# A decoder of twelve sublayers on one core: scan outputs summed by TensorE, l3's attention lagged, l2's down products in one block, statistics where x is completed, latent folds by transposes

## The reference

```python
def _layernorm(x, axis=-1, eps=1e-05):
    m = jnp.mean(x, axis=axis, keepdims=True)
    v = jnp.var(x, axis=axis, keepdims=True)
    return (x - m) / jnp.sqrt(v + eps)

# L1_attn: a selective scan over 256 positions, 96 channels, 16 states
def step(x, inp):
    dA_t, dBu_t, C_t = inp
    x = dA_t * x + dBu_t
    y = jnp.einsum('bdn,bn->bd', x, C_t)
    return (x, y)
# ... the result is y + u * Dp

# L2_xattn, L3_xattn: 16 heads of latent attention. The weights alone give, head by head,
# a matrix Am (Wq, w_kc_q, W_qr, W_kr) for the queries and Bm (w_kc_kv, Wo) for the outputs.
```

## Time and profile before

| | |
|---|---|
| device time, median of 3 runs | 3240.33 us (3240.13 to 3252.0) |
| the profiled execution | 3245.44 us, its span 3243.6 us |
| TensorE / VectorE / ScalarE / GpSimd busy | 78% / 55% / 30% / 25% |
| mean granted TensorE clock | 0.829 of full |
| layer norms start at (us) | 7, 129, 274, 493, 731, 1158, 1296, 2116, 2444, 2565, 2713, 3039 |
| l1 attention; its scan | 493 to 731; 578.6 to 722.4 |
| folds of l2's and l3's latent attention | 2126.5 to 2170.2; 2723.9 to 2767.5 |
| l2 feed-forward's down products | 2534.7 to 2564.8 |
| l3 attention, from first scores to last addition | 2601.5 to 2713.2 |

### The profile page before, as it was taken

How to read it: one execution, slowest core, us unless ns; L and a number is a source line. 1 busy time by engine, 2 the same in 40 slices (tenths; PEclk the granted TensorE clock), 3 DMA queues, 4 the chain that set the end, 5 groups by cost and what they waited for, 6 DMA issues and landing times. The chain is left out here.

```text
span 3243.6 us, 37597 instructions
## 1 busy us (share of the span) xinstructions
PE 2533.6 (78%) x14342; PEld 1696.4 (52%) x14342; DVE 1770.8 (55%) x3533; ACT 985.2 (30%) x2219; POOL 814.6 (25%) x586
## 2 busy tenths in 40 slices
PE   7784443668999979569778697779998666999899
PEld 4563321224345556448666475765558545555555
DVE  5347586994455533674847657425556544355411
ACT  3131011541045521233342343405552011355311
POOL 1210001220058832100100000007880000488322
PEclk8886555669999989687978788779999856999899
DMA  1000000003000010210000001030001003000311
GB/s 32 20 16 20 0 1 13 0 0 98 1 1 1 1 53 1 107 24 1 14 14 13 14 1 26 1 91 1 1 1 39 19 1 91 1 1 1 96 44 37
DMA packets 96554, 72.86 MB, mean 22 GB/s; under 512 B 51232, under 2 KB 89936, under 8 KB 95801
## 3 DMA queue, kind: packets, MB, share of 16 engines
q1 hardware_dynamic: 95353, 69.01, 7.6%
q0 software_dynamic: 1024, 1.45, 0.2%
HBM read 65.17 MB, written 5.28 MB: 22 GB/s over the span
## 5 line engine op out<-in xcount | busy, mean ns | idle before, releaser
L1964 POOL TENSOR_SCALAR work<-work,small 128x512 f32<-128x512 f32 x384 | 594.0, 1565 | 809.1 <-DVE small L1900 809.1
L1942 ACT ACTIVATE work<-psum,small 128x512 f32<-128x512 f32 x384 | 260.5, 683 | 251.9 <-DVE small L1895 251.9
L1895 DVE TENSOR_REDUCE small<-psum 128x2 f32<-128x1024 f32 x192 | 234.9, 1225 | 179.0 <-PE psum L1845 178.9
L1845 PE MATMUL psum<-keysT,arena_a 64*128 64x512 f32 x768 | 218.2, 647 | 9.1 <-ACT work L1942 6.2
L1855 PEld LDWEIGHTS psum<-consts,work 128*128 128x128 f32 x1536 | 164.9, 141 | 114.3 <-issue 102.5
L1867 PE MATMUL psum<-work,keys 128*64 128x256 f32 x1536 | 187.0, 384 | 36.1 <-issue 34.2
L1855 PE MATMUL psum<-consts,work 128*128 128x128 f32 x1536 | 211.1, 280 | 4.4 <-DVE work L1906 2.6
L1867 PEld LDWEIGHTS psum<-work,keys 128*64 128x64 f32 x1536 | 120.0, 136 | 136.0 <-issue 110.0
L2753 PE MATMUL psum<-xnT,arena_a 128*128 128x256 f32 x512 | 154.7, 463 | 29.3 <-DVE arena_b L3133 29.3
L1489 PE MATMUL psum<-arena_b,arena_a 96*96 96x512 f32 x128 | 93.3, 898 | 71.9 <-DVE arena_b L1518 37.5
L2753 PEld LDWEIGHTS psum<-xnT,arena_a 128*128 128x128 f32 x512 | 117.0, 236 | 55.9 <-DVE arena_b L3133 31.5
(11 more groups left out here) (582 smaller groups left out, 5122.7 us busy)
## 6 DMA issues: line engine op xcount, KB each, us to landing
arena_a<-in_L_xattn_Wo SPq DMA_DIRECT2D x3, 2048.0 KB, 13.4
arena_a<-in_L_xattn_Wq SPq DMA_DIRECT2D x3, 2048.0 KB, 18.2
arena_a<-in_L_xattn_w_kc_q SPq DMA_DIRECT2D x3, 1536.0 KB, 12.8
arena_a<-in_L_attn_w_qkv SPq DMA_DIRECT2D x1, 4096.0 KB
arena_a<-in_L_xattn_W_qr SPq DMA_DIRECT2D x3, 768.0 KB
arena_b<-in_L_ffn_w_fc SPq DMA_DIRECT2D x1, 2048.0 KB
arena_b<-in_L_ffn_w_proj SPq DMA_DIRECT2D x1, 2048.0 KB
arena_a<-in_L_attn_w_gate SPq DMA_DIRECT2D x1, 2048.0 KB
```

The source lines that it names most:

```text
L1845: mm = nc.tensor.matmul(ps[:, u % 2 * 2 + j, :], qT[r:r + DC, p, t * P:(t + 1) * P], k.keysT[r:r + DC, b * SK:(b + 1) * SK], start=True, s ...
L1895: nc.vector.tensor_reduce(top[:, 2 * u:2 * u + 2], ps[:, u % 2 * 2:u % 2 * 2 + 2, :], AX.X, ALU.max, negate=True).then_inc(*maxed.up())
L1942: nc.scalar.activation(probs[u % NPB][:, j, :], ps[:, u % 2 * 2 + j, :], ACT.Exp, bias=top[:, i:i + 1], accum_out=total[:, i:i + 1]).then_ ...
L1964: nc.gpsimd.tensor_scalar(probs[u % NPB][:, j, :], probs[u % NPB][:, j, :], total[:, i:i + 1], None, ALU.mult).then_inc(*scaled.up())
```

## The change

1. `statistics` takes the statistics of a tile right behind the addition that completes it, in the block of the sublayer before; `layernorm` starts with the aggregation (the first stage keeps its own).
2. In l1's scan TensorE sums the sixteen products and u * D into two PSUM banks by an identity matrix; GpSimd's block is gone. B and C columns are spread one by one over three pairs of banks.
3. In the folds without rope Dm and Am are made transposed, with 64-column weights and 128 or 256 columns streamed, and turned by 8 and 16 transposes. w_qc loads in the layer norm, w_kc_kv and Wo last, and Bm is made last.
4. l2's down products move into the block of the steps; additions take two tiles at once.
5. l3's loop is lagged by one more item for transposes and sums, with three buffers for the probabilities. ScalarE takes the copy of the transposed probabilities and the squares; VectorE weighs the sums as it takes them from PSUM. Root, scaling and output projection follow in the same block by pairs of tiles. The lambda steps come first in the projection block.

```diff
+def statistics(k, dve, tiles, done):
+    dve.wait_ge(*done)
+    for t in tiles:
+        k.nc.vector.bn_stats(k.ln_stats[:, t, :], k.x[:, t, :]).then_inc(*k.sig("ln_stats").up())
 def layernorm(k, interleave=False, fetch=None, first=False):
-            for t in range(NT):
-                last = nc.vector.bn_stats(st[:, t, :], x[:, t, :])
-            k.link(dve, last, "dve")
+            if first:
+                for t in range(NT):
+                    nc.vector.bn_stats(st[:, t, :], x[:, t, :]).then_inc(*k.sig("ln_stats").up())
+            dve.wait_ge(k.sig("ln_stats").sem, k.sig("ln_stats").total)
...
 # l1_attn, scan, TensorE
+            def spread(r):
+                s, g = divmod(r, 2)
+                if r >= 3:
+                    pe.wait_ge(*(read if (r - 3) % 2 else taken).at((r - 3) // 2 + 1))
+                w = w_x[:, R + g * NS + s:R + g * NS + s + 1].broadcast_to([C, C])
+                for n in range(2):
+                    mm = nc.tensor.matmul(ps[0:C, r % 3 * 2 + n, :], w, u[:, n * 512:(n + 1) * 512], start=True, stop=True)
+                mm.then_inc(*bred.up())
+            def collect(s):
+                if s >= 0:
+                    pe.wait_ge(*read.at(s + 1))
+                for n in range(2):
+                    mm = nc.tensor.matmul(ps[0:C, y_banks[n], :], k.c["ident"][0:C, 0:C], hC[s % 2][:, n * 512:(n + 1) * 512],
+                                          start=s < 0, stop=s == NS - 1)
+                mm.then_inc(*added.up())
+            for r in range(2):
+                spread(r)
+            collect(-1)
             for s in range(NS):
...
+                for r in (2 * s + 2, 2 * s + 3):
+                    if r < 2 * NS:
+                        spread(r)
+                collect(s)
-        @block.gpsimd
-        def _(pool):
-            for s in range(NS):
-                pool.wait_ge(*read.at(s + 1))
-                nc.gpsimd.tensor_tensor(y, y, hC[s % 2], ALU.add).then_inc(*added.up())
-                pool.wait_ge(*added.at(s + 1))
+            dve.wait_ge(*added.at(NS + 1))
+            nc.vector.tensor_copy(y.rearrange("p (a b) -> p a b", a=2), ps[0:C, 6:8, :])
...
 # latent_attention, folds without rope, TensorE
+                for hp in range(HP):
                     for c in range(2):
-                        mm = nc.tensor.matmul(ps[:, h // 8, h % 8 * DC:(h % 8 + 1) * DC], w_qc[:, h, c, :],
-                                              Cm[:, c_at(h), c, :], start=c == 0, stop=c == 1)
+                        for j in range(2):
+                            h = 2 * hp + j
+                            mm = nc.tensor.matmul(ps[j * DC:(j + 1) * DC, 4 + hp // 4, hp % 4 * K:(hp % 4 + 1) * K],
+                                                  Cm[:, c_at(h), c, :], w_qc[:, h, c, :], start=c == 0, stop=c == 1)
+                pe.wait_ge(*taken.at(2))
+                for hp in range(HP):
+                    mm = nc.tensor.transpose(ps[:, 6 + hp // 4, hp % 4 * P:(hp % 4 + 1) * P], DmT[:, hp, :], k.c["ident"])
                 pe.wait_ge(*taken.at(3))
-                        mm = nc.tensor.matmul(ps[:, 2 + col // 512, col % 512:col % 512 + DC],
-                                              wq[:, h, c * P:(c + 1) * P], Dm[:, h, :], start=True, stop=True)
+                    mm = nc.tensor.matmul(ps[r:r + DC, hp // 2, hp % 2 * D:(hp % 2 + 1) * D], Dm[:, h, :], wq[:, h, :],
+                                          start=True, stop=True)
+                pe.wait_ge(*taken.at(4))
...
+                outputs(0)
...
 # l2_ffn, TensorE, after the steps and in their block
+            pe.wait_ge(*used.at(len(steps) - 1))
+            for t in range(NT):
+                pe.wait_ge(*ready.at(t // 2 * 2 + 2))
+                for j in range(G * R):
+                    mm = nc.tensor.matmul(ps[:, t // 2, t % 2 * D:(t % 2 + 1) * D], hs[:, j // R, j % R, t * P:(t + 1) * P],
+                                          wd[:, j // R, j % R, :], start=j == 0, stop=j == G * R - 1)
...
 # l3_attn, the loop: TensorE, ScalarE, VectorE
-            for m in range(M + 2):
+            for s in range(M + 3):
+                if s < M:
+                    scores(s)
+                if 2 <= s <= M + 1:
+                    turn(s - 2)
+                if s >= 3:
+                    over_keys(s - 3)
+            for b in range(B + 1):
+                if b < B:
+                    turn_out(b)
+                if b >= 1:
+                    project(b - 1)
...
+            for s in range(M + 4):
+                if s < M:
+                    exps(s)
+                if 2 <= s <= M + 1:
+                    keep(s - 2)
+                if s >= 4:
+                    square(s - 4)
+            nc.scalar.activation(ss, ss, ACT.Sqrt, bias=k.c["eps5"], scale=1.0 / HW).then_inc(*rooted.up())
+            for b in range(B):
+                keep_out(b)
...
+            for s in range(M + 3):
+                if s < M:
+                    row_max(s)
+                if 1 <= s <= M:
+                    mix(s - 1)
+                if s >= 3:
+                    weigh(s - 3)
```

267 lines of the change are left out of this document (145 added, 122 removed).

## The result

The changed kernel takes 3124.3 us (median of 4 runs, 3117.0 to 3126.2) against 3244.2 us before on the same chip: a ratio of 0.9624, 95% interval 0.9597 to 0.9650. The prediction was 3120 us. The profiled execution took 3123.0 us, its span is 3121.2 us and the mean granted clock 0.855 (before 0.829).

The account below looks back on a forecast made before the run. No single bound was taken: each changed stretch was priced by the wait that ends last. Savings of 9.7 + 17.3 + 31.4 + 18.8 + 43.2 = 120.4 us off 3245.4, less 5.1 to the median, gave 3120 us (3095 to 3145).

Parts of the forecast that it names:

- l2's down products: l2's feed-forward: down products run under VectorE's last two steps and end at 2545.3 instead of 2564.3, saving 18.8 us.
- l3's attention: l3's attention: the lag cuts an item from 5.74 to 3.15 us; with the lambda steps moved, 43.2 us saved.
- Layer norms: Eleven layer norms start with the aggregation: 8 save 2.16 us and 3 save 2.75, 25.5 us in all.
- the last pairs: Statistics behind the last additions before each layer norm lie on the path, costing 8.8 us in all.
- I expose a third: Inner statistics steps in l0 and l2 attention and three latent stages: a third counted as unhidden, 4 us.
- Scan: l1's scan: without GpSimd's addition a step falls from 8.55 to 7.4 us; 17.3 us saved in sum.
- rival (1): l1's scan: TensorE at half clock becomes the bound, a step takes 10.3 us, kernel 3188 us; chance 0.07.
- Rival (4): l1's scan: L200 is long for another reason than GpSimd's addition; 18 us more, kernel 3138 us; chance 0.02.
- Folds: Latent-attention folds in l2 and l3: each falls from 43.7 to 28 us, 31.4 us saved for both.
- rival (2): Latent-attention folds: only they stay at half clock, 36.3 us instead of 28, kernel 3136 us; chance 0.10.
- Rival (3): l3's loop: squares between exponentials cost ScalarE two table switches an item; 22 us more, kernel 3142 us; chance 0.05.
- Rival (5): Latent loops: delayed by statistics, they keep a longer rhythm; at 0.68 us a unit the kernel takes 3250; chance 0.02.

Follow-up runs that it names:

- stats_ln: The changed kernel with all statistics steps put back at the start of the layer norms: 3121.0 us, ratio 0.9624.
- beside: The changed kernel with an unread GpSimd addition of 96x1024 put beside each of the first fifteen scan steps: 3127.5 us, ratio 0.9647.
- l0_late: The changed kernel with the statistics of a pair in l0's attention moved behind the next gating in VectorE's queue: 3104.6 us, ratio 0.9580.
- l3_fill: l0_late with two needless products of 128 rows and 256 columns per item in l3's attention loop, ahead of the sums: 3098.7 us, ratio 0.9564.
- warm_all: l0_late with four needless 512-column products on TensorE at the start of every layer norm but the first: 3115.1 us, ratio 0.9604.

## Why the prediction was right, and where it wasn't

The total (3120 against 3124.3) is right, in part by luck. Of its terms four are right or nearly so. Stepping from before over stats_ln to the changed kernel, by the profiles: scan, folds with the queries, down products and l3's attention gave 115.6 us (110.7 forecast), everything else 10.9 (none forecast, 9.9 of them in the delta rule), the statistics -4.1 (9.7 forecast): 122.4, where 120.4 was forecast. Errors of 14 us one way and 16 the other met in the middle.

- **Layer norms.** 25.5 us forecast, 24.9 measured; the table load is late next, as stated, and takes 1.28 us.
- **What the statistics cost elsewhere: mis-sized in one block, missed in two, open in sum.** I counted 8.8 for the last pairs and 7 for the inner steps. Against stats_ln 28 us came back by the medians and 25 by the ratios, not 15.8, so the net of 9.7 came out as 0 to -3; by the three other kernels with the same steps it is 9 to 11. Where I costed a step by its own duration I was right: l0's feed-forward lost 2.7 (3.2). The step that failed is "I expose a third": in l0's attention three steps of 0.8 us stand ahead of the gating, and TensorE, arriving later, gets the half clock more often. They mostly cost 6 to 8 us between the first addition and the last, where a third would be 0.8. And one cost had no term at all: the shorter layer norm leaves less time to its loads, which took 3.0 us in l2's feed-forward and 1.1 in l3's projections.
- **Scan.** 17.3 forecast, 18.2 measured. L200 gave 16.9 (17.8 forecast), a step takes 7.30 us (7.4), the start gained 1.8 (1.9). TensorE's cover held; its clock rose to 0.90, and rival (1) didn't come. Rival (4) is refuted by beside.
- **Folds.** 31.4 forecast, 16.9 and 11.8 measured, 28.8. In l2 the block takes 26.8 us (28): its transposes, 16 in 1.97 us with a granted clock of 1.00, run at nearly twice the speed that 16 have at half clock in the earlier trace rows. So the rule of the Trainium skill ("TensorE: Matmul & The Clock Gate", Part 4, PE-mode transpose), that the full clock does not engage for transposes, doesn't hold here. In l3 31.8, since the clock was at half from 2612.3, in the layer norm, to 2632.8: part of rival (2), but not by its reason, for the clock fell before any fold ran. w_kc_q was "just in time": 2.4 us late. The queries gained 4.5 us, which I had named as up to 3 and not counted.
- **l2's down products.** 18.8 forecast. The products end 10.8 us behind the last mask (11 named). Without the statistics (stats_ln) the block falls by 19.1, with them by 15.9. Of the 3.2 us between the two 0.75 are the last steps, which I had counted, and 2.5 are there ahead of the masks already: TensorE's first product waits 3.0 us longer for the load. In l0_late these are 1.3 and 1.7. No run has this change by itself; the rows of this block are all there is for it.
- **l3's attention.** 43.2 forecast, 40.9 measured (41.7 with the last pair's 0.8 us, counted above, put back; 43.0 in stats_ln, whose projections don't wait for their load). The item was mis-sized: 3.48, not 3.15 us, for I took 0.35 us off the scores as a drain that the next instruction covers, and their 2.01 us count in full. The first three items are faster than the rhythm, so the sixteenth started 46.9 us into the loop (47.2 forecast); from there to the last addition it took 23.2 us, not 21.3. Rival (3) is refuted: one table load in the loop's tail, none inside.
- **Rival (5).** The latent loops grew by 3.1 us in all, 0.016 us a unit.
- **What no term had.** Code that nobody touched takes other times: cross attention +5.4, l2's first block +3.4, delta rule -6.1, l3's feed-forward -3.6. In sum -0.9 us here; in the profiles of beside and l0_late the same four are 12.5 and 14.4 us below before, and the delta rule alone ranges over 12 us. A total that comes out within 4 us owes something to luck.

## What to carry over

Count a step that is put into a queue by who waits for the instruction behind it, and put work of its kind behind the instruction that the bounding engine waits for; here three steps of 0.8 us cost 6 to 8. Before a pause is shortened, look which loads land in it. Where an item's chain bounds a loop in which no engine is full, a lag of one more item breaks it: without it nothing of the gain was left. Moving a load ahead is part of a faster block: the new order of three loads was worth 15 us, and where the clock made l3's folds faster, the wait for the same load grew instead (3.9 us in l3_fill, 5.2 in warm_all).

## What the runs showed of the hardware

- A GpSimd addition that reads SBUF holds up VectorE's three-operand step in SBUF: 2.5 us instead of 1.28, until the addition is over; VectorE's product with a PSUM operand beside it isn't touched (1.21 us).
- l3's loop had the half clock for 46 us with TensorE busy all the time. With 1.0 us of products over all rows added to each item the granted clock was 1.00 and the item fell from 3.48 to 2.74 us; with a quarter of those columns it stayed at half. Whether it is the rows or the mere amount of work that counts was not separated.
- Blocks of the same code take different courses of the clock in kernels that differ elsewhere: 114.5 to 122.8 us for one block, 769 to 782 for another. Single blocks of single profiles are to be compared with that in mind; two profiles that agree up to the edit (beside and l0_late, 0.03 us apart) make the safer pair.
- Sixteen float32 transposes take 1.97 us at a granted clock of 1.00 and 3.65 us at 0.50.
